# A residual block with two 3x3 convolutions: x's column sum formed by DMA, conv 2's inner planes rounded and split together

## What is computed

```python
identity = x
out = jax.nn.relu(_bn(_conv3x3(x, w1, stride=1), g1, b1, m1, v1))
out = _bn(_conv3x3(out, w2, stride=1), g2, b2, m2, v2)
return jax.nn.relu(out + identity)
```

## Time and profile before

| | |
|---|---|
| median of 3 runs | 596.51 us (595.66 to 597.7) |
| the profiled execution, its own time | 596.25 us |
| its span in the trace | 594.3 us |
| PE busy | 576.5 us, 97% |
| weight loads (beside PE) | 533.7 us, 90% |
| DVE busy | 555.3 us, 93% |
| ACT busy | 472.6 us, 80% |
| POOL busy | 19.8 us, 3% |
| chain that ended last | PE 93% |

### The profile page before, as it was taken

One profiled execution on the slowest core, in us unless ns is written; L12 is line 12 of the kernel. 1 busy time (PEld: TensorE's weight loads), 2 busy tenths in 40 slices (PEclk: granted clock), 3 DMA queues, 4 the chain that ended last, 5 costly groups with the idle time before them and its releaser, 6 DMA issues.

```text
span 594.3 us, 8667 instructions
## 1 busy us (share of the span) xinstructions
PE 576.5 (97%) x2962; PEld 533.7 (90%) x2962; DVE 555.3 (93%) x475; ACT 472.6 (80%) x730; POOL 19.8 (3%) x28
## 2 busy tenths in 40 slices
PE   6769999999999999999999999999999999999997
PEld 3769999999999999999999999999999999999996
DVE  6899999999999999999999999999999999999963
ACT  5687888887788887788887778888778888778874
POOL 7500000000000000000000000000000000000000
PEclk9799999999999999999999999999999999999999
DMA  4112223322223331232332222332122233121012
GB/s 161 56 61 88 104 84 110 112 82 82 83 83 110 110 108 56 83 109 84 110 110 67 89 92 83 110 110 93 71 83 93 100 110 110 58 82 51 29 55 108
DMA packets 22458, 53.23 MB, mean 90 GB/s; under 512 B 1584, under 2 KB 18096, under 8 KB 22448
## 3 DMA queue, kind: packets, MB, share of 16 engines
q1 hardware_dynamic: 22304, 52.80, 25.0%
q10 hardware_dynamic: 144, 0.29, 0.2%
HBM read 27.40 MB, written 25.69 MB: 89 GB/s over the span
## 4 chain that ended last, share of the span: by engine, by line
PE 93%; DVE 2%; ACT 1%; issue 0%; POOL 0%
PE psum L639 93%; DVE x_outer L367 1%; DVE x_lo L375 1%; DVE psum L389 1%; ACT w_mat L488 0%; DVE t_outer L412 0%; POOL g_t L181 0%; ACT psum L514 0%; DVE t_inner L398 0%; DVE x_inner L355 0%; ACT out_sb L563 0%; ACT z L534 0%; ACT z L535 0%; DVE x_inner L359 0%
## 5 line engine op out<-in xcount | busy, mean ns | idle before, releaser
L639 PE MATMUL psum<-x_hi,w_hi 128*128 128x392 f32 (+2 forms) x512 | 175.3, 342 | 6.7 <-DVE x_lo L375 6.7
L639 PE MATMUL psum<-x_hi,w_lo 128*128 128x392 f32 (+2 forms) x512 | 175.8, 343 | 0.0
L639 PE MATMUL psum<-x_lo,w_hi 128*128 128x392 f32 (+2 forms) x512 | 175.1, 342 | 0.0
L389 DVE TENSOR_TENSOR psum<-psum,z 128x784 f32<-128x784 f32 (+1 forms) x128 | 127.1, 993 | 21.3 <-ACT hidden L540 9.9
L639 PEld LDWEIGHTS psum<-x_hi,w_hi 128*128 128x128 f32 x512 | 97.0, 189 | 8.3 <-issue 4.8
L639 PEld LDWEIGHTS psum<-x_hi,w_lo 128*128 128x128 f32 x512 | 97.0, 189 | 0.4
L639 PE MATMUL psum<-t_inner,w_mat 128*128 128x392 f32 x256 | 94.7, 492 | 2.7 <-ACT psum L514 2.7
L639 PEld LDWEIGHTS psum<-x_lo,w_hi 128*128 128x128 f32 x512 | 97.0, 189 | 0.4
L563 ACT ACTIVATE out_sb<-psum 128x784 f32<-128x784 f32 x64 | 52.8, 825 | 47.1 <-PE psum L639 47.0
L639 PE MATMUL psum<-h_lo,w_hi 128*128 128x392 f32 x256 | 87.3, 341 | 0.0
L639 PE MATMUL psum<-h_hi,w_hi 128*128 128x392 f32 x256 | 87.2, 341 | 0.0
(11 more groups left out here) (67 smaller groups left out, 747.5 us busy)
## 6 DMA issues: line engine op xcount, KB each, us to landing
x_sb<-x_dram SPq DMA_DIRECT2D x32, 814.0 KB, 4.3
out_dram<-out_sb SPq DMA_DIRECT2D x64, 392.0 KB, 2.8
w_raw<-w_dram ACTq DMA_DIRECT2D x1, 288.0 KB, 3.5
w_raw<-w_dram SPq DMA_DIRECT2D x1, 288.0 KB, 5.4
bn<-params_dram SPq DMA_DIRECT2D x1, 132.0 KB, 3.7
```

What stands on the lines that cost most here:

```text
L389: nc.vector.tensor_tensor(psum[:, half, EVEN:ODD + 1, 0:width], t1, z[:, half, :, 0:width], ALU.add).then_inc(joined[conv], 1)
L639: ins = nc.tensor.matmul(psum[:, half, bank, first:first + (j1 - j0) * WQ], w[:, i, far, :], moving, start=not onto and at == 0, stop=at = ...
```

## The change

**Column sum of x.** DVE's `sum_x` is gone. SP loads the even columns of image n a second time, straight into `x_inner[:, k, 0]` (`load_even`), and POOL, once they have landed, issues a DMA that adds the odd columns onto them in place (`add_odd`, `accum_op=ALU.add`). ACT's rounding of the inner planes waits for the mark `summed`. The planes `x_inner` and `x_outer` now hold rows of 29 values, 28 of which are used, and the DVE and ACT instructions read or write 28 of 29 where they need to; the outer difference works on whole runs of 812 values.

**Conv 2's difference plane.** It is rounded and split like the others, in one instruction with the sum plane: `t1_hi`, `t1_lo` become `ti_hi`, `ti_lo` with two planes. DVE writes sum and difference, then marks both ready together; ACT rounds both in one instruction; DVE takes both rests in one; PE waits for the rests and the residual ahead of the difference product, which is three passes now.

**Also.** `x_hi` and `x_lo` lose their two border rows, and with them POOL's eight small memsets, since conv 1's matmuls never read them. The raw filters share memory with `z` and `out_sb`. Four steps instead of two at the end are outside the loop. In the last image's step the halves of the new split are placed by hand. POOL's rests of conv 2's weights are taken in its step 0, between two of its DMAs.

```diff
-        x_outer = sb("x_outer", [P, 2, NQ, WQ])
-        x_inner = sb("x_inner", [P, TBUFS, 2, NQ, WQ])
-
-        x_hi = sb("x_hi", [P, 2, 4, NQ + 2, WQ], F32R)
-        x_lo = sb("x_lo", [P, 2, 4, NQ + 2, WQ], F32R)
+        x_outer = sb("x_outer", [P, 2, RUN])
+        x_inner = sb("x_inner", [P, TBUFS, 2, RUN])
+
+        x_hi = sb("x_hi", [P, 2, 4, NQ, WQ], F32R)
+        x_lo = sb("x_lo", [P, 2, 4, NQ, WQ], F32R)
...
-        t1_hi = sb("t1_hi", [P, NP, WQ], F32R)
-        t1_lo = sb("t1_lo", [P, NP, WQ], F32R)
+        ti_hi = sb("ti_hi", [P, 2, NP, WQ], F32R)
+        ti_lo = sb("ti_lo", [P, 2, NP, WQ], F32R)
...
+        even_in = [sem(f"even_in{i}") for i in range(TBUFS)]
+        summed = [sem(f"summed{i}") for i in range(TBUFS)]
...
-            with eng.Fori(0, (N - 4) // 4) as turn:
+            with eng.Fori(0, (N - 8) // 4) as turn:
                 for k in range(4):
                     step(turn * 4 + (2 + k), (2 + k) % 4)
-            for s in range(N - 2, N + 2):
+            for s in range(N - 6, N + 2):
...
+        def runs(cells, first, step):
+
+            return cells[:, first:first + 2 * step].rearrange("p (s r) -> p s r", s=2)[:, :, 0:RUN]
 
         def x_full(which, k):
 
             full, places = (x_outer[:], slice(0, 2)) if which == "outer" else (x_inner[:, k], slice(2, 4))
-            return full.rearrange("p s j q -> p s (j q)"), places
+            return full.rearrange("p s (j c) -> p s j c", c=WQ + 1)[:, :, :, 0:WQ], places
...
-            if which == "t1":
-                return t_inner[:, 0, rows], t1_hi[:, rows], t1_lo[:, rows]
+            if which == "inner":
+                return t_inner[:, :, rows], ti_hi[:, :, rows], ti_lo[:, :, rows]
...
+            def load_even(n, k):
+
+                sp.dma_start(x_inner[:, k, 0], x_rows[n][:, 0:RUN]).then_inc(even_in[k], 16)
+
             sp.dma_start(bn[:], params).then_inc(bn_in, 16)
             load(sp, 0, 0)
-            sp.dma_start(w_raw[2][:], w2).then_inc(w_in[2], 16)
+            load_even(0, 0)
+            sp.dma_start(w_raw[2], w2).then_inc(w_in[2], 16)
+            load(sp, 1, 1)
+            load_even(1, 1)
+
+            load_even(2, 2)
 
             def step(s, k):
-                if not isinstance(s, int) or s + 2 < N:
+                if not isinstance(s, int) or 0 <= s < N - 2:
 
                     wait(sp, tx_ready["outer"], s + 3 - XBUFS)
                     load(sp, s + 2, k + 2)
                 if there_is(s, s - 2):
                     store(s - 2, 0)
                     store(s - 2, 1)
+                if not isinstance(s, int) or 0 <= s < N - 3:
+
+                    wait(sp, res_ready, 2 * s)
+                    load_even(s + 3, (k + 3) % 4)
...
-            for t in (x_hi, x_lo):
-                for b in range(2):
-                    for row in (0, NQ + 1):
-                        nc.gpsimd.memset(t[:, b, :, row, :].bitcast(F32), 0.0).then_inc(zeroed, 1)
             nc.gpsimd.memset(hidden[:], 0.0).then_inc(zeroed, 1)
             nc.gpsimd.memset(wmat[2][:], 0.0).then_inc(mat_zeroed, 1)
...
+            def add_odd(n, k):
+
+                pool.wait_ge(even_in[k], (n - k) * (16 // TBUFS) + 16)
+                odd = x_rows[n][:, XPLANE + 1:XPLANE + 1 + RUN]
+                pool.dma_start(x_inner[:, k, 0], odd, accum_op=ALU.add).then_inc(summed[k], 16)
+
+            add_odd(0, 0)
...
-            low_weights(pool, "all2")
+
+            def step(s, k):
+                if is_step(s, 0):
+                    low_weights(pool, "all2")
+                if there_is(s, s + 2):
+
+                    add_odd(s + 2, (k + 2) % 4)
+
+            run(pool, step)
...
-            def sum_x(n, k):
-
-
-                dve.wait_ge(x_in[k % XBUFS], (n - k % XBUFS) * (16 // XBUFS) + 16)
+            def difference_x(n, k):
+
+                dve.wait_ge(x_in[k % XBUFS], until(n, k))
                 wait(dve, res_ready, 2 * (n - TBUFS) + 2)
-                nc.vector.tensor_tensor(x_inner[:, k, 0], x_columns(k, 0), x_columns(k, 1), ALU.add)
-
-            def difference_x(n, k):
-
-                nc.vector.tensor_tensor(x_inner[:, k, 1], x_columns(k, 1), x_columns(k, 0),
+                cells = runs(x_sb[:, k % XBUFS], 0, XPLANE + 1).rearrange("p s (j c) -> p s j c", c=WQ + 1)
+                nc.vector.tensor_tensor(x_full("inner", k)[0][:, 1], cells[:, 1, :, 0:WQ], cells[:, 0, :, 0:WQ],
                                         ALU.subtract).then_inc(tx_ready["inner"], 1)
 
             def outer_x(n, k):
 
-
                 wait(dve, xlo_ready["outer"], n)
-                cells = x_planes(k, XPLANE)
-                nc.vector.tensor_tensor(x_outer[:], cells[:, :, :, 0:WQ], cells[:, :, :, 1:WQ + 1],
+                cells = x_sb[:, k % XBUFS]
+                nc.vector.tensor_tensor(x_outer[:], runs(cells, 0, XPLANE), runs(cells, 1, XPLANE),
                                         ALU.subtract).then_inc(tx_ready["outer"], 1)
...
-                wait(dve, inner[2], 4 * n)
+                wait(dve, hlo_ready["inner"], n)
                 nc.vector.tensor_tensor(t_inner[:, 0, rows], hid_data[:, 0, rows, 0:WQ], hid_data[:, 1, rows, 0:WQ],
-                                        ALU.add).then_inc(th_ready["t1"], 1)
+                                        ALU.add)
 
             def difference_hidden(n, half=None):
 
                 rows = hidden_rows(half)
                 nc.vector.tensor_tensor(t_inner[:, 1, rows], hid_data[:, 1, rows, 0:WQ], hid_data[:, 0, rows, 0:WQ],
-                                        ALU.subtract).then_inc(th_ready["t2"], 1)
+                                        ALU.subtract).then_inc(th_ready["inner"], 1)
...
+                    split_hidden("inner", N - 1, kl % 2, 0)
                     sum_hidden(N - 1, 1)
+                    difference_hidden(N - 1, 1)
                     join(2, N - 2, 1, before_conv2(N - 2))
-                    split_hidden("t1", N - 1, kl % 2, 0)
                     split_hidden("outer", N - 1, kl % 2, 0)
                     outer_hidden(N - 1, 1)
-                    difference_hidden(N - 1, 1)
-                    split_hidden("t1", N - 1, kl % 2, 1)
+                    split_hidden("inner", N - 1, kl % 2, 1)
...
-                if ahead:
-                    sum_x(s + 1, ka)
-                if last:
-                    split_hidden("t1", s - 1, kl % 2)
+                if last:
+                    split_hidden("inner", s - 1, kl % 2)
                 if ahead:
...
+                if which == "inner":
+                    act.wait_ge(summed[k], (n - k) * (16 // TBUFS) + 16)
...
-                wait(act, *((inner[2], 4 * n) if which == "t1" else (outer[2], 2 * (n - 1))))
+                wait(act, *((inner[2], 4 * n) if which == "inner" else (outer[2], 2 * (n - 1))))
...
-                    high_hidden("t1", s - 1, kl % 2)
+                    high_hidden("inner", s - 1, kl % 2)
...
-                if (conv, i) == (2, 2):
-                    return ((t_inner[:, 1], wmat[2]),)
...
-                elif i == 1:
-                    hi, lo = t1_hi, t1_lo
+                elif i in (1, 2):
+                    hi, lo = ti_hi[:, i - 1], ti_lo[:, i - 1]
...
-                pe.wait_ge(th_ready["t2"], n + 1 + more)
+                pe.wait_ge(hlo_ready["inner"], n + 1 + more)
                 pe.wait_ge(res_ready, 2 * n + half + 1)
                 sum_products(2, half, 2, SUM_T2, passes_of(2, 2, 0), True).then_inc(inner[2], 1)
-
-                pe.wait_ge(hlo_ready["t1"], n + 1 + more)
                 sum_products(2, half, 1, SUM_T1, passes_of(2, 1, 0), True).then_inc(inner[2], 1)
```

More of the change, by code:

```diff
@@ L31, in residual_block @@
     WQ = W // 2
-    assert P == 128 and N % 4 == 0
+    assert P == 128 and N % 4 == 0 and N > 8
     HALF1 = ((0, (NP + 1) // 2), ((NP + 1) // 2, NP))
@@ L40, in residual_block @@
     XPLANE = NQ * (WQ + 1) + 1
+    RUN = NQ * (WQ + 1)
     with ExitStack() as ctx:
@@ L65, in residual_block, with scratch @@
         out_sb = sb("out_sb", [P, 2, 2, (NQ // 2) * WQ])
-        w_raw = {1: sb("w1_raw", [P, 3, 3, C]), 2: sb("w2_raw", [P, 3, 3, C])}
+        spare = {1: z[:].rearrange("p h s r -> p (h s r)"), 2: out_sb[:].rearrange("p h s r -> p (h s r)")}
+        def scratch(conv, at, kinds):
+            size = kinds * 3 * C
+            return spare[conv][:, at:at + size].rearrange("p (k h c) -> p k h c", k=kinds, h=3)
+        w_raw = {conv: scratch(conv, 0, 3) for conv in (1, 2)}
         bn = sb("bn", [P, 8 + 4 * C])
@@ L75, in residual_block @@
         bias = sb("bias", [P, 2])
-        g_t = {1: sb("g1_t", [P, 4, 3, C]), 2: sb("g2_t", [P, 4, 3, C])}
-        g_sum = {1: sb("g1_sum", [P, 3, C]), 2: sb("g2_sum", [P, 3, C])}
+        g_t = {conv: scratch(conv, 9 * C, 4) for conv in (1, 2)}
+        g_sum = {conv: scratch(conv, 21 * C, 1)[:, 0] for conv in (1, 2)}
         wmat = {1: sb("w1_mat", [P, 4, 2, P]), 2: sb("w2_mat", [P, 4, 2, P])}
@@ L111, in residual_block @@
```

(21 more changed lines are left out.)

15 lines of the change are left out of this document (6 added, 9 removed).

## The result

Before: 596.09 us, the median of four runs. After: 612.79 us (612.13 to 613.7). The ratio is 1.0277, with a 95% interval of 1.025 to 1.0303: slower by 2.8%. The profiled execution after took 612.13 us with a span of 610.5.

What follows compares the result with a forecast made beforehand. PE was taken to bound the kernel at 17.62 us per step, with DVE late by little. Profiled 596.25 + 12.7 (loop) - 0.8 (tail) + 0.8 (start) = 608.95, forecast 609 us, range 596 to 616.

Steps and rivals of the forecast that it cites:

- PE saves 0.48 us per image: Conv 2's difference plane on PE: rounded products replace fp32, saving 0.24 us per half; PE alone would need 17.14 us per step.
- DVE's work is unchanged: DVE per step: dropped column sum (0.88 us) traded for the wider split and outer difference, together +0.02 us.
- The wait of DVE's join for ACT, 0.82 us: Conv 1's first join waits for ACT's ReLU behind the doubled rounding: 3.49 us after the difference starts, against 2.67.
- The loop, 18.02 us: Round through DVE's join and split, PE's four groups and ACT's ReLUs: 18.02 us per step against 17.62.
- PE idle for 0.9 us per step: PE stands idle ahead of conv 2's first rounded inner product, released by DVE's split; busy share about 92%.
- Sum: Joins of step 1 to 31: thirty rounds of 18.02 us are 540.6 us, against 527.94, so +12.7.
- The tail: Last one and a half steps, without a new image: PE saves 0.96 us less 0.15 for its later start, -0.8.
- The start, +0.8: POOL's scaled-weights chain begins later, behind an accumulating DMA that awaits the even columns: +0.8 us, ends -0.5 and +3.
- rival D: Accumulating DMA lands late and ACT waits before rounding x; needs over 30 us per transfer; chance 0.08 with Rival C.
- Rival A: PE stays the bound and the 0.48 us of 31 images comes out: 582 us, faster; chance 0.09.
- B: Only the DVE and ACT round counts, the way through PE closing under 17.60 us: 596.3 us; chance 0.09.
- Rival C: POOL's DMA work stops DVE, 1 us per image costing 18 us: 627 us; chance 0.08 together with rival D.

Runs made afterwards that it cites:

- e9_round_two: Changed kernel, conv 2's inner planes each rounded and split alone, difference first; on ACT the output ReLU stands between both roundings: 585.26 us, ratio 0.9819.
- e7_extra_in_chain: Changed kernel plus one 392-element ACT copy per step between the rounding of the inner planes and the output ReLU: 625.85 us, ratio 1.0498.
- e3_relu_first: Changed kernel with the output ReLU of s-2, half 0, moved on ACT ahead of the rounding of conv 2's inner planes: 594.46 us, ratio 0.9981.
- e10_round_two_start: e9_round_two with the column sums of images 0 and 1 on DVE, so POOL's first accumulating DMA is image 2's: 583.28 us, ratio 0.9783.
- e6_and_first_sums_on_dve: Changed kernel with output ReLU ahead of the rounding, split in two, and column sums of images 0 and 1 on DVE: 589.25 us, ratio 0.9891.
- e4_split_two: Changed kernel with DVE's doubled split in two instructions, difference plane first, PE waiting for that one alone before its first group: 596.53 us, ratio 1.001.
- e1_part_dma: Changed kernel keeping the column sum by DMA, but with conv 2's difference plane as fp32 product as before: 597.68 us, ratio 1.0023.
- e2_part_split: Changed kernel keeping the three passes and doubled split, but with the column sum back on DVE and no added DMA: 639.52 us, ratio 1.0721.

## Why the prediction was right

It said 609 us (596 to 616) and "slower" at 0.81; measured were 612.8. The mechanism of the loop was the one named, step by step; that of the start was so only in part:

- **PE saves 0.48 us per image.** Right in the main: `e9_round_two`, which lets PE run, has steps of 17.21 us against 17.60, 0.39 less.
- **DVE's work is unchanged.** Right: the 1624-element split takes 1.84 us as costed, and strided or run-wise reads cost nothing here (`x_outer` 1.84 us, as the split of the same 1624 elements; the difference of x 0.97, as before).
- **The wait of DVE's join for ACT, 0.82 us.** 0.73 and 0.65 us in the rows. From the start of the difference to the join 3.41 us instead of 3.49: ACT took over at once (325.99 to 326.02) where 0.11 was assumed. `e7_extra_in_chain` and `e3_relu_first` show it as a cause.
- **The loop, 18.02 us.** 18.08, term by term: join to PE 2.85 (2.90), PE's four groups 8.68 (8.54), to the ReLU 0.20 (0.20), to the next join 1.14 (1.09), join and sum 1.80 (1.80), then 3.41 (3.49). The mis-sized term is PE's. After the wait its first matmul is 0.28 us ahead of the next instead of 0.178, which is most of the 0.14.
- **PE idle for 0.9 us per step.** The rows name 0.75 and 0.67 us behind the modelled ends; from start to start, less the pace of 0.178, the pauses are 0.91 and 0.82 us (312.08 to 313.17, 330.24 to 331.24), plus 0.10 for that slow first matmul; PE busy at 93% where 92% was said.
- **Sum.** 543.20 us between the joins instead of 540.6: 2.6 of the missing 3.2 us against the profiled execution. The tail came out at -0.74 instead of -0.8.
- **The start, +0.8.** +1.68, inside the ends but for another reason in part. POOL was released at 8.01 (7.8 expected), and the issue took 1.00 us; PE's first product came 0.94 us later (18.64 against 17.70). Of these, 0.4 us stay when the addition is gone: in `e10_round_two_start` POOL's chain still begins at 7.97 instead of 7.63, and PE's first product comes at 18.09. The rest is the step as put. What set the join of step 1 was **image 1**: POOL got to its addition only at 24.36, behind the filters, the data landed at 29.5, and ACT waited 3.34 us for them; the chain that ended last passes through this transfer. That is rival D, dismissed because a transfer has 35 us. In the loop it has; at the start, before a lead is built up, it had 1.8 us, from POOL's issue to 26.20, where ACT was free. The sentence to be corrected is "It needs over 30 us per transfer". `e6_and_first_sums_on_dve` and `e10_round_two_start` give the price of both images' additions: 2 us. That +1.68 lay within the ends was luck in part, for an older delay went away in its place: before, POOL's work had stretched `x_outer` to 3.88 us, and in `e10_round_two_start` it did so again (3.52 us), with the join of step 1 at 36.94, where it was before (36.91). From POOL's issue to the landing of 406 KB, the addition included, it was 5.1 us in the median of 32 transfers, against 3.2 for as many bytes from SP; what part of this is the issue, the transfer or the addition is not separated by any run.
- **Rival A, 582 us,** was the price of a PE that stays the bound. The change didn't reach it; `e9_round_two` came to 585.3 and `e10_round_two_start` to 583.3. **B**, 596.3 with a step of 17.60, is what `e4_split_two` came to (596.5, 17.60); that `e3_relu_first` ended near it is chance, its step being the length of another loop.
- **Rival C.** Refuted: DVE's operations at 320.02 and 320.91 lie beside POOL's issue at 320.48 and take 0.97 and 1.78 us, as without it (0.98 and 1.79 in the earlier trace rows). `e1_part_dma`, with the same 32 issues, has a step of 17.59 us, like before (17.60). The 1 us per image by which its price supposed DVE to be held stands in no row and was shown by no run; POOL's issue at 320.48 took 0.88 us.

## What to carry to other kernels

Ask of every instruction that gets longer what stands behind it in its engine's list, and who waits for that: a rounding that starts one DVE operation later and takes 0.7 us longer is nothing to an ACT that is 80% busy, and ahead of the ReLU it cost 18 us, because that ReLU releases another engine's buffer. Follow the release round to where it began; only the longest loop counts, and when you reorder, price the loop that the new order closes before you count the gain. Then look for what else the waiting engine waits for: once the split was early, the residual came last. A transfer that is hidden in the loop may be bare in the first images, as that of image 1 was here, for 3.34 us.

## What was unexpected of the hardware

- After its wait in the loop PE's first matmul was followed late: 0.28 us from start to start (313.17, 331.24) where 0.178 is the pace, at a granted clock of 1.00 (0.45 us in the record at 313.17 instead of 0.34). In `e2_part_split` it was 0.28 and 0.29 us (309.47, 328.47).
- In `e2_part_split` a pause of PE of 3.0 us (40.52 - 37.36 less a pace) was followed by a granted clock of 0.50 from 40 to 46 us, and that step took 2.7 us more than the later ones. That the pause lowered the clock is not shown: it was 0.70 already from 34 to 38 us. From 300 to 400 us, with shorter pauses (1.61 us ahead of 309.47, 1.64 ahead of 328.47), it was 1.00. The first matmul behind the long pause:

```profile
40.52 0.66 PE L658 MATMUL psum<-ti_hi,w_hi 128*128 128x392 f32 x1 [2.84 <-DVE ti_lo L438]
```

- POOL and DVE, both reading two SBUF operands: in the start of every profiled execution the one that began first kept its speed, and the other took longer. Before, POOL began at 25.93 and took 2.41 us, DVE at 26.11 took 3.88. After, the order was the other one:

```profile
26.19 1.84 DVE L396 TENSOR_TENSOR x_outer<-x_sb 128x1624 f32<-128x1624 f32 x1
```

  DVE kept its 1.84 us and POOL, from 26.29, took 3.97. POOL's 2.41 us and the 1.74 that DVE still had to go are 4.15. In `e10_round_two_start` POOL was first again (25.91, 2.41 us), and DVE was the one that took longer:

```profile
26.51 3.52 DVE L402 TENSOR_TENSOR x_outer<-x_sb 128x1624 f32<-128x1624 f32 x1
```

  Over the twelve executions: where POOL began first (six), it took 2.39 to 2.41 us and DVE 3.48 to 3.88, but for `e6_and_first_sums_on_dve`, where it began at 25.28 beside DVE's difference (24.76 to 25.73) and took 2.69, and DVE 3.15. Where DVE began first (six), it took 1.84 and POOL 3.95 to 3.97.
